# Causal cut of the diagonal tiles: a mask matmul on TensorE, or a select on GpSimd

## The chip, the cores and the metric

The kernel runs on one core of a Trainium2 chip. The metric is the device time in microseconds (us) of one execution; lower is better. The profile is one execution taken by the hardware profiler; its span runs from the first to the last instruction.

## What is computed

A token array of 2 batch rows x 1024 tokens x 128 features goes first through one attention layer of 16 heads of 8 features with its MLP (the opening of the kernel), and then through four decoder layers. Each of these has causal attention with 16 query heads and 4 key/value heads of 64 features and a mixture of 8 experts of which each token takes 2. Only the causal attention of the four layers is touched here:

```python
x = hidden_states
for l in range(L):                                   # L = 4, NH = 16, NKV = 4, HD = 64
    h = _rms(x, ln1_w[l])
    q, k, v = ...                                    # projections, rotary on q and k
    k = jnp.repeat(k, rep, axis=1); v = jnp.repeat(v, rep, axis=1)
    scores = jnp.einsum('bhqd,bhkd->bhqk', q, k) / jnp.sqrt(HD)
    scores = scores + causal_bias                    # 0 for k <= q, -1e9 for k > q
    attn = jax.nn.softmax(scores, axis=-1)
    out = jnp.einsum('bhqk,bhkd->bhqd', attn, v)
    x = jnp.clip(x + out.transpose(...).reshape(...) @ wo[l], -100, 100)
    x = jnp.clip(x + _moe(_rms(x, ln2_w[l]), ...), -100, 100)
```

## The kernel before

**Tiling.** A layer has `HEADS` = 8 passes: 4 key/value heads for each of 2 batch rows. A pass treats `GQ` = 4 query heads together. Its 1024 queries are 8 tiles of 128 (`t`), its keys 8 tiles of 128 (`kt`), and only `kt <= t` is computed: 36 steps a pass, of which 8 are diagonal (`kt == t`). Over 4 layers this is 1152 steps with 256 diagonal ones.

**A step.** `scores2` on TensorE writes the scores of 128 keys x (4 heads x 128 queries) into one of two PSUM banks `psS` with two matmuls (L1782, L1783); the row maximum is already among the operands. On a diagonal step a third matmul (L1785) adds the bf16 mask `maskk` through an identity, -1e9 where the key is later than the query. ScalarE takes the exponential (L1415) into `prob`, a ring of four SBUF buffers of 128x512 fp32. TensorE multiplies it by the values (`values`, L1799) into `psO`. GpSimd adds the tiles of a query tile up into `psum_k` for the denominator (L1217, shown as xw): one addition for each step with `kt > 0`. After the last step of a query tile TensorE spreads the sum with a matmul by ones (`denominator`, L1814), VectorE inverts it and scales (L2084, L2086), TensorE applies the output projection (`out_projection`, L1821) and VectorE adds the result (L2205). For `t == 0` the denominator reads `prob` directly.

**Beside it** runs work for the passes that follow: projections (L1725 to L1727), rotary sums on GpSimd (L1234), their low parts (L1243), and row maxima (L1754 with their own mask `maskq`, L1757, and the reductions L2110 on VectorE). These take the other four PSUM banks. After a layer's attention come the experts, which overlap its last pass.

**What sets the order.** Each engine runs its instructions in a fixed order. `network_order` describes every step as a stage with an engine, a cost in ns and the stages that it follows; `planned` walks through them as a list scheduler with 150 ns for a handover between engines and 110 ns for a turn of TensorE between 64-column work (kinds V and D) and the rest, and the program is written out in that order. So a changed cost or dependency moves the work of all engines. The opening is planned apart, and `opening_order` is not touched. In the tables of names, `S` is a step's scores on TensorE, its exponential on ScalarE and its addition on GpSimd; `V` the values, `D` the denominator, `O` the output projection, `M` the maxima.

**Waits.** `s_ex` counts exponentials, `s_su` GpSimd's additions, `s_pv` values, `s_qk` scores, `s_dn` denominators. An exponential waits for its scores and for the values and the addition of the step four before, which read the same buffer of `prob`.

## Time and profile before

| | us |
|---|---|
| median of 3 runs | 3364.86 |
| lowest and highest | 3364.70, 3366.26 |
| the profiled execution | 3365.88 |
| its span | 3364.0 |

The opening takes the first 640 us; the four layers follow. The profile is read from its share of busy time by engine, then by stretches within a layer, then by the chain of work that ended last, and last by the single instructions that the change removes or adds. A matmul's duration in the profile covers its way through the array, so that of matmuls that follow each other closely each one's own cost is the distance from one end to the next; the chain shows this distance.

### The profile page before, as it was taken

What the parts mean: (1) busy time and instruction counts of PE and PEld (TensorE: products, weight loads), DVE (VectorE), ACT (ScalarE), POOL (GpSimd) and SP (SyncE); (2) the same over time, 40 slices, a digit from 0 to 9 for tenths busy, and PEclk for the clock granted to TensorE, in tenths of its full rate; (3) what the DMA queues carried; (4) which work ended last, traced back from release to release, by engine and by line L of the source; (5) the groups of instructions that cost most, each with busy time, mean ns of one, the idle gap of its engine ahead of it and who ended that gap; (6) DMA issues with size and microseconds to landing.
All of it is one profiled execution on the core that took longest, in us unless ns stands there. A gap on an engine that the chain in (4) does not pass through costs nothing.

```text
span 3364.0 us, 51431 instructions
## 1 busy us (share of the span) xinstructions
PE 3165.4 (94%) x17792; PEld 2097.7 (62%) x17792; DVE 2568.0 (76%) x3764; ACT 1706.8 (51%) x3085; POOL 2009.9 (60%) x1573
## 2 busy tenths in 40 slices
PE   5999998799999999999999999999999999999998
PEld 3555554566666677666666776666667766666576
DVE  6778775777887777878876778778867888788667
ACT  4566667444435475444344755443446553443465
POOL 2101000378778665778776657787776577876765
PEclk8899999899999999999999999999999999999999
DMA  5433412333322155332231553232215532232153
GB/s 121 78 67 62 81 45 43 77 85 68 75 61 67 46 172 134 82 73 64 67 73 32 181 138 85 61 76 67 61 30 188 141 90 61 67 76 61 27 175 116
DMA packets 160401, 283.60 MB, mean 84 GB/s; under 512 B 32592, under 2 KB 64208, under 8 KB 159888
## 3 DMA queue, kind: packets, MB, share of 16 engines
q1 hardware_dynamic: 159632, 280.18, 33.4%
q8 instruction: 145, 2.38, 0.3%
q14 instruction: 112, 0.92, 0.1%
q10 hardware_dynamic: 512, 0.13, 0.0%
HBM read 88.47 MB, written 31.72 MB: 36 GB/s over the span
## 4 chain that ended last, share of the span: by engine, by line
PE 52%; DVE 6%; ACT 3%; issue 2%; POOL 1%; DMA 1%; SPq 0%; DVEq 0%; ACTq 0%
PE psA L1799 11%; PE psA L1782 7%; PE psA L1754 6%; PE psA L1783 5%; PE psA L1826 3%; PE psA L1827 3%; PE psA L1828 3%; PE psA L1814 3%; DVE rden L2084 2%; PE psA L1821 2%; DVE mxp L2110 2%; PE psA L1863 1%; PE psA L1757 1%; PE psA L1864 1%; PE psA L1865 1%
## 5 line engine op out<-in xcount | busy, mean ns | idle before, releaser
L1415 ACT ACTIVATE prob<-psA 128x512 f32<-128x512 f32 x1152 | 652.6, 595 | 1045.6 <-PE psA L1783 460.2
L1217 POOL TENSOR_TENSOR xw<-xw,prob 128x512 f32<-128x512 f32 x672 | 867.9, 1291 | 232.3 <-ACT prob L1415 158.5
L2110 DVE TENSOR_REDUCE mxp<-psA 128x1 f32<-128x512 f32 (+3 forms) x864 | 528.5, 663 | 57.1 <-PE psA L1754 35.2
L2084 DVE RECIPROCAL rden<-psA 128x256 f32<-128x256 f32 x256 | 448.8, 1753 | 131.9 <-PE psA L1814 125.5
L1782 PE MATMUL psA<-qs,ks 128*128 128x512 f32 x1152 | 524.8, 456 | 18.7 <-ACT prob L1415 17.4
L1754 PE MATMUL psA<-ks,qs 128*128 128x512 f32 (+3 forms) x1536 | 476.6, 387 | 11.8 <-DVE mxp L2110 5.7
L1251 POOL TENSOR_TENSOR hidl<-gate,hidh 128x512 fp32r<-128x512 f32 x256 | 331.2, 1302 | 211.4 <-ACT hidh L1470 209.6
L1783 PE MATMUL psA<-qs,ks 128*128 128x512 f32 x1152 | 454.6, 395 | 0.0
L1217 POOL TENSOR_TENSOR xw<-prob 128x512 f32<-128x512 f32 x224 | 287.7, 1284 | 274.0 <-issue 129.8
L2032 DVE TENSOR_REDUCE mxp<-psA 128x1 f32<-128x1024 f32 x256 | 304.7, 1220 | 83.7 <-PE psA L1590 82.7
L1334 ACT ACTIVATE pr<-psA 128x512 f32<-128x512 f32 x512 | 274.3, 602 | 140.1 <-PE psA L1609 122.9
L1754 PEld LDWEIGHTS psA<-ks,qs 128*128 128x128 f32 x1536 | 270.7, 193 | 84.8 <-issue 31.8
L1782 PEld LDWEIGHTS psA<-qs,ks 128*128 128x128 f32 x1152 | 221.1, 192 | 140.0 <-issue 67.4
L1799 PE MATMUL psA<-prob,vv 128*64 128x256 f32 x2304 | 292.2, 387 | 6.5 <-DVE inner L2205 3.7
L1799 PE MATMUL psA<-prob,outer 128*64 128x256 f32 x2304 | 293.6, 386 | 5.0 <-DVE inner L2205 5.0
L2110 DVE TENSOR_REDUCE mxq<-psA 128x1 f32<-128x384 f32 (+3 forms) x352 | 209.7, 637 | 105.0 <-PE psA L1757 103.0
L1234 POOL TENSOR_TENSOR rab<-rab,rbp 128x512 f32<-128x512 f32 x192 | 247.4, 1303 | 36.5 <-DMA rbp<-rab 36.5
L2236 DVE TENSOR_TENSOR gate<-psA,spread 128x512 f32<-128x512 f32 x256 | 175.9, 687 | 101.5 <-ACT psA L1464 100.4
L1163 POOL TENSOR_TENSOR feat<-feat,smr 128x1024 f32<-128x1024 f32 x16 | 30.6, 1915 | 360.3 <-DVE smr L2015 360.3
L1783 PEld LDWEIGHTS psA<-qs,ks 128*128 128x128 f32 x1152 | 219.0, 190 | 21.3
L1826 PE MATMUL psA<-xh,eh 128*128 128x512 f32 x512 | 211.4, 413 | 17.9 <-DVE gate L2236 10.4
L1799 PEld LDWEIGHTS psA<-prob,vv 128*64 128x64 f32 x2304 | 155.1, 137 | 104.1 <-issue 25.6
(222 smaller groups left out, 5839.0 us busy)
## 6 DMA issues: line engine op xcount, KB each, us to landing
qs<-normed SPq DMA_DIRECT2D x256, 256.0 KB, 4.1
rbp<-rab SPq DMA_DIRECT2D x256, 192.0 KB, 3.5
spread<-routing_weights SPq DMA_DIRECT2D x128, 256.0 KB, 3.6
qs<-qs SPq DMA_DIRECT2D x64, 256.0 KB, 3.2
expert_weight_halves<-eh SPq DMA_DIRECT2D x32, 384.0 KB, 2.5
expert_weight_halves<-el SPq DMA_DIRECT2D x32, 384.0 KB, 3.6
eh<-expert_weight_halves SPq DMA_DIRECT2D x32, 384.0 KB, 3.2
el<-expert_weight_halves SPq DMA_DIRECT2D x32, 384.0 KB, 3.9
```

The source lines that it names most:

```text
L1217: g.tensor_tensor(psum_k[:, t % 2, :], before, prob[:, i % 4, :], ALU.add).then_inc(s_su, 1 if kt > 1 else 2 + (t == 1))
L1251: g.tensor_tensor(hidl[:, n % 3, :], gate[:, n % GATES, :], hidh[:, n % 3, :], ALU.subtract).then_inc(s_hl, 1)
L1334: act(pr1[:, j % 2, h, :], psS1[:, n % 3, :], ACT.Exp).then_inc(s_ex1, 1)
L1415: act(prob[:, k % 4, :], psS[:, k % 2, :], ACT.Exp, scale=float(HD) ** -0.5).then_inc(s_ex, 1)
L1754: ins = mm(bank[:, i, :], qs1[b][:, c, h + i, t % TPC * P:(t % TPC + 1) * P], ks[b][:, 0, k0:k1], start=(i == 0), stop=not diagonal)
L1782: mm(psS[:, i % 2, :], ks[b][:, 0, tile], qs1[b][:, c, :, qs], start=True, stop=False)
L1783: ins = mm(psS[:, i % 2, :], ks[b][:, 1, tile], qs2[b][:, c, :, qs], start=False, stop=(kt < t))
L1799: ins = mm(psO[t % 2][q * HD:(q + 1) * HD, 0:256], vv[b][:, kt, g * HD:(g + 1) * HD], prob[:, i % 4, q * 256:(q + 1) * 256], start=(kt == ...
L1826: mm(dst, eh[held(w)][:, w0:w0 + P], xh[:, cs], start=True, stop=False)
L2032: vec.tensor_reduce(mxp1[:, p % 2, c, h * 4 + t:h * 4 + t + 1], pair("M", p, c, t, h), AX.X, ALU.max).then_inc(s_mx1, 1)
L2084: vec.reciprocal(rden[:, :], psO[t % 2][:, 256:512]).then_inc(s_rd, 1)
L2110: vec.tensor_reduce(dst, bank, AX.X, ALU.max).then_inc(s_mr, 1)
```

## The change

The diagonal step loses its mask matmul (and `maskk` its setup). After the exponential GpSimd sets the entries of later keys to zero in place, with an `affine_select` over the 128 x (4 x 128) tile: a new stage `Sd` for each of the 256 diagonal steps, with a cost of 900 in the plan. The values of a diagonal step, its addition, and the denominator of `t == 0` now wait for this select through a new semaphore `s_sd2`. The row maximum (`maskq`) stays as it is.

```diff
-        stage("tensor", ("S", l, n, t, kt), 440 + 100 * (kt == t), ("land", ("J", l, n, t // TPC)) if kt == 0 else None,
+        stage("tensor", ("S", l, n, t, kt), 440, ("land", ("J", l, n, t // TPC)) if kt == 0 else None,
               back("scalar", "S", 2), *first)
         stage("scalar", ("S", l, n, t, kt), 600, ("tensor", ("S", l, n, t, kt)), back("tensor", "V", 4), back("gpsimd", "S", 4))
-        stage("gpsimd", ("S", l, n, t, kt), 1390 * (kt > 0), ("scalar", ("S", l, n, t, kt)),
-              tile("tensor", "D", 2) if kt == 1 else None)
+        if kt == t:
+            stage("gpsimd", ("Sd", l, n, t), 900, ("scalar", ("S", l, n, t, t)))
+        whole = ("gpsimd", ("Sd", l, n, t)) if kt == t else ("scalar", ("S", l, n, t, kt))
+        stage("gpsimd", ("S", l, n, t, kt), 1390 * (kt > 0), whole, tile("tensor", "D", 2) if kt == 1 else None)
         if t == 0:
-            stage("tensor", ("D", l, n, t), 500, ("scalar", ("S", l, n, 0, 0)), tile("vector", "O", 2), *early)
-        stage("tensor", ("V", l, n, t, kt), 460, ("scalar", ("S", l, n, t, kt)),
+            stage("tensor", ("D", l, n, t), 500, whole, tile("vector", "O", 2), *early)
+        stage("tensor", ("V", l, n, t, kt), 460, whole,
...
+                elif what == "Sd":
+                    l, n, t = i
+                    it, k = l * HEADS + n, TRI[t] + t
+                    g_.wait_ge(s_ex, it * TRI[TPB] + k + 5)
+                    cut = prob[:, k % 4, :].rearrange("p (h n) -> p h n", h=GQ)
+                    g.affine_select(out=cut, in_=cut, compare_op=ALU.is_ge, fill=0.0, base=0,
+                                    pattern=[[0, GQ], [1, P]], channel_multiplier=-1).then_inc(s_sd2, 1)
...
+                    if kt == t:
+                        g_.wait_ge(s_sd2, it * TPB + t + 1)
...
-                ins = mm(psS[:, i % 2, :], ks[b][:, 1, tile], qs2[b][:, c, :, qs], start=False, stop=(kt < t))
-                if kt == t:
-                    ins = mm(psS[:, i % 2, :], identb[:, :], maskk[:, :].unsqueeze(1).broadcast_to([P, GQ, P]), start=False, stop=True)
-                ins.then_inc(s_qk, 1)
+                mm(psS[:, i % 2, :], ks[b][:, 1, tile], qs2[b][:, c, :, qs], start=False, stop=True).then_inc(s_qk, 1)
...
                 t_.wait_ge(s_ex, it * TRI[TPB] + i + 5)
+                if kt == t:
+                    t_.wait_ge(s_sd2, it * TPB + t + 1)
...
-                    t_.wait_ge(s_ex, it * TRI[TPB] + 5)
+                    t_.wait_ge(s_sd2, it * TPB + 1)
```

The plan comes out in another order. GpSimd in the second layer, pass 5, before: query tiles 4 and 5 (L1217 additions, L1234 rotary sums, L1243 low parts).

```order
L1217 TENSOR_TENSOR xw<-prob 128x512
L1217 TENSOR_TENSOR xw<-xw,prob 128x512 x3
L1234 TENSOR_TENSOR rab<-rab,rbp 128x512 x2
L1217 TENSOR_TENSOR xw<-prob 128x512
L1217 TENSOR_TENSOR xw<-xw,prob 128x512 x4
L1243 TENSOR_TENSOR qs_0<-rab,normed 128x512 x2
```

The same place after the change. L1208 is the select; the additions are now L1225, the rotary sums L1242, the low parts L1251.

```order
L1225 TENSOR_TENSOR xw<-prob 128x512
L1225 TENSOR_TENSOR xw<-xw,prob 128x512 x2
L1208 AFFINE_SELECT prob<-prob 128x512
L1225 TENSOR_TENSOR xw<-xw,prob 128x512
L1242 TENSOR_TENSOR rab<-rab,rbp 128x512
L1225 TENSOR_TENSOR xw<-prob 128x512
L1225 TENSOR_TENSOR xw<-xw,prob 128x512
L1242 TENSOR_TENSOR rab<-rab,rbp 128x512
L1225 TENSOR_TENSOR xw<-xw,prob 128x512 x2
L1208 AFFINE_SELECT prob<-prob 128x512
L1225 TENSOR_TENSOR xw<-xw,prob 128x512
L1251 TENSOR_TENSOR qs_0<-rab,normed 128x512
```

Each query tile's last addition has a select right ahead of it, and rotary sums that stood in pairs are spread between additions.

TensorE at the diagonal step of query tile 4 in the same pass, before: from the scores of key tile 4 to the values (L1799) that read them.

```order
L1782 MATMUL psA<-qs_1,ks 128x512
L1783 MATMUL psA<-qs_1,ks 128x512
L1785 MATMUL psA<-maskk,identb 128x512
L1782 MATMUL psA<-qs_1,ks 128x512
L1783 MATMUL psA<-qs_1,ks 128x512
L1821 MATMUL psA<-wos,att 128x128 x2
L1754 MATMUL psA<-ks,qs_0 128x384
L1757 MATMUL psA<-maskq,identb 128x128
L1799 MATMUL psA<-prob,vv 64x256 x12
L1782 MATMUL psA<-qs_1,ks 128x512
```

The end of the same piece after the change (scores are L1790 and L1791, maxima L1762 and L1765, values L1806, denominator L1821 there). The diagonal scores stand 22 rows above the values, with the output projection, three further steps of scores and seven pieces of maxima between them.

```order
L1762 MATMUL psA<-ks,qs_0 128x384
L1765 MATMUL psA<-maskq,identb 128x128
L1762 MATMUL psA<-ks,qs_0 128x512
L1765 MATMUL psA<-maskq,identb 128x128
L1762 MATMUL psA<-ks,qs_0 128x512
L1765 MATMUL psA<-maskq,identb 128x128
L1762 MATMUL psA<-ks,qs_0 128x512
L1765 MATMUL psA<-maskq,identb 128x128
L1762 MATMUL psA<-ks,qs_0 128x512
L1765 MATMUL psA<-maskq,identb 128x128
L1806 MATMUL psA<-prob,vv 64x256 x12
L1821 MATMUL psA<-xw,ones 64x256 x2
```

The values of the diagonal step moved back behind other work, and the denominator joined them in one run of 64-column matmuls.

## Rows read from the trace of the kernel before

**Rows 1.** The page: busy time by engine, then shares in 40 slices.

```profile
PE 3165.4 (94%) x17792; PEld 2097.7 (62%) x17792; DVE 2568.0 (76%) x3764; ACT 1706.8 (51%) x3085; POOL 2009.9 (60%) x1573
...
PE   5999998799999999999999999999999999999998
...
PEclk8899999899999999999999999999999999999999
```

**Rows 2.** Busy time in two stretches of attention: start:end, length, PE, PEld, DVE, ACT, POOL.

```profile
1340.00:1840.00 500.00, 484.10 (x2982) 316.95 (x2981) 388.84 (x596) 215.20 (x394) 374.23 (x294) 1.00 0.27 63
```

```profile
2000.00:2480.00 480.00, 464.60 (x2823) 308.07 (x2821) 384.70 (x588) 207.94 (x377) 356.77 (x280) 1.00 0.28 65
```

**Rows 3.** The chain that ended last within 1340 to 1840 us, shares by line.

```profile
by line: PE psA L1799 24.7%; PE psA L1782 14.8%; PE psA L1783 11.6%; PE psA L1754 11.5%; PE psA L1814 5.5%; DVE rden L2084 3.8%; PE psA L1821 3.8%; DVE mxp L2110 3.4%; PE psA L1757 2.5%; PE psA L1785 2.5%; issue 2.3%; PE psA L1725 1.8%; PE 
```

**Rows 4.** The mask matmul L1785 within 1340 to 1840 us: PE busy and count.

```profile
1340.00:1840.00 500.00, 24.27 (x62) 5.99 (x62) 1.00 0.27 63
```

**Rows 5.** The chain within 1400 to 1440 us in time: start, own cost in us, what.

```profile
1407.30 0.28 PE psA L1782
1407.58 0.24 PE psA L1783
1407.82 0.23 PE psA L1785
...
1427.81 1.88 PE psA L1799 x16
1429.69 0.43 PE psA L1814 x4
1430.12 0.43 PE psA L1782
1430.55 0.24 PE psA L1783
1430.79 0.23 PE psA L1782
```

**Rows 6.** GpSimd by line and form: count, busy us, mean ns, idle before.

```profile
L1217 POOL TENSOR_TENSOR xw<-xw,prob 128x512 f32<-128x512 f32 x672 | 867.9, 1291 | 232.3 <-ACT prob L1415 158.5 <-POOL xw L1217 1.3
...
L1190 POOL COPY outer<-vtok 128x256 f32<-128x256 f32 x8 | 3.2, 398 | 30.3 <-PE psA L1620 21.8 <-ACT vtok L1301 8.4
...
L1179 POOL MEMSET order<- 128x1 f32 x8 | 0.3, 99 | 0.0
...
L1149 POOL TENSOR_SCALAR_AFFINE_SELECT ident<-ident 128x128 f32<-128x128 f32 x1 | 0.3, 292 | 0.2 <-POOL ident L1147 0.2
...
L1185 POOL TENSOR_SCALAR_AFFINE_SELECT maskk<-maskk 128x128 bf16<-128x128 bf16 x1 | 0.3, 292 | 0.0
```

**Rows 7.** In order of time: start us, us, engine, line, idle before and its releaser.

```profile
863.83 1.08 ACT L1415 ACTIVATE prob<-psA 128x512 f32<-128x512 f32 x2 [4.86 <-PE psA L1799]
864.51 1.29 POOL L1217 TENSOR_TENSOR xw<-xw,prob 128x512 f32<-128x512 f32 x1 [4.11 <-ACT prob L1415]
...
870.61 0.39 PE L1785 MATMUL psA<-maskk,identb 128*128 128x512 bf16 x1
...
871.04 0.60 ACT L1415 ACTIVATE prob<-psA 128x512 f32<-128x512 f32 x1 [0.87 <-PE psA L1785]
```

**Rows 8.** Who waited for whom over the whole span: us, times, longest.

```profile
ACT prob L1415 <- PE psA L1799: 323.1, 139, 5.1
...
PEld psA L1821 <- DVE att L2086: 45.0, 55, 1.6
...
ACT prob L1415 <- POOL xw L1217: 28.9, 39, 2.6
...
PEld psA L1799 <- ACT prob L1415: 28.9, 72, 1.4
```

More of the change, by code:

```diff
@@ L641, in network_order @@
              "Ew", "Eh", "El", "Es", "Er", "Hf", "Hw", "Hh", "Hl", "Si", "Y", "Ug", "Uu", "Aw", "Wa", "Wb",
-             "W", "K", "H", "R", "Q", "J", "A", "X", "L", "D", "O", "V", "S", "P", "M", "Zk", "Za", "Zb", "Zs", "Zv", "Zd", "Zi", "Zr", "Zo"]
+             "W", "K", "H", "R", "Q", "J", "A", "X", "L", "D", "O", "V", "Sd", "S", "P", "M", "Zk", "Za", "Zb", "Zs", "Zv", "Zd", "Zi", "Zr", "Zo"]
     return planned(plan, kinds, 150, 150, "VD", 110, {"vector": 120})
@@ L690, in program @@
         maskq = sb("maskq", [P, P], BF16)
-        maskk = sb("maskk", [P, P], BF16)
         ones64 = sb("ones64", [P, HD])
@@ L841, in program @@
         s_rw = [sem(f"max2_in_stack_{c}") for c in range(NCH)]
+        s_sd2 = sem("diagonal_cut")
         s_qk, s_ex, s_su, s_pv = sem("scores2"), sem("exp2"), sem("probabilities_summed"), sem("pv2")
@@ L861, in program @@
         PV_FREE = 2 * TPB + 2
-        N_CS2 = 4 + E + 3
+        N_CS2 = 3 + E + 2
         ROWS_DONE = scaled(4, 3) + 1
@@ L1174, in opening @@
                         g.memset(maskq[:, :], 0.0).then_inc(s_cs2, 1)
-                        g.memset(maskk[:, :], 0.0).then_inc(s_cs2, 1)
                         g.memset(ones64[:, :], 1.0).then_inc(s_cs2, 1)
@@ L1179, in opening @@
                             g.memset(order[:, e:e + 1], float(E - e)).then_inc(s_cs2, 1)
-                        g_.wait_ge(s_cs2, 4 + E)
+                        g_.wait_ge(s_cs2, 3 + E)
                         g.affine_select(out=identb[:, :], in_=identb[:, :], compare_op=ALU.not_equal, fill=1.0, base=0,
@@ L1184, in opening @@
                                         pattern=[[-1, P]], channel_multiplier=1).then_inc(s_cs2, 1)
-                        g.affine_select(out=maskk[:, :], in_=maskk[:, :], compare_op=ALU.is_ge, fill=NEG, base=0,
-                                        pattern=[[1, P]], channel_multiplier=-1).then_inc(s_cs2, 1)
                     if p > 1:
```

## The prediction

> **What bounds the kernel now.** I read the page first, for the share of each engine. TensorE is busy 94% of the span and at full granted clock in nearly all slices after the opening; no other engine is above 76% [rows 1]. An average can hide a stage with another limit, so the next view is the busy time by stretches inside the attention of two layers. In 1340 to 1840 us TensorE works 484.1 of 500 us (97%), VectorE 388.8 (78%), GpSimd 374.2 (75%), ScalarE 215.2 (43%) [rows 2]; in 2000 to 2480 us the shares are 97, 80, 74 and 43%. So here TensorE has 3% of idle time and GpSimd 25%. Busy matmuls may still be waiting ones, so the third view is the chain that ended last in this stretch: mostly matmuls, with VectorE's reciprocal at 3.8% and its maxima at 3.4%, GpSimd nowhere among the first lines, and the mask matmul L1785 itself at 2.5% [rows 3]. This is the picture of an engine that is the bound by its own issue: time taken from it comes off the end, unless something else steps in at once.
>
> **The matmuls removed.** There are 256 of them (4 layers x 8 passes x 8 diagonal steps). Their duration in the windows is 24.27 us for 62 [rows 4], 0.39 us each, but that is the way through the array; in the chain each costs 0.23 us, as the score matmuls beside it do [rows 5]. 256 x 0.232 = 59.4 us of TensorE's time (0.232 is the middle distance between the ends of L1783 and L1785 over the 256 pairs, [rows 5] rounds it). How much of that is on the path: L1785 has 2.5% of 500 us in the chain [rows 3], 12.5 us, where its 62 instances [rows 4] cost 62 x 0.232 = 14.4 us. So 87% is on the path: 59.4 x 0.87 = 51.6 us. The rest ran in the shadow of a chain through VectorE. I take 51.6, and 59.4 as the upper bound.
>
> What another rule would make of this term: the Trainium skill, "TensorE: Matmul & The Clock Gate", section "Back-to-back issue gap", gives about 131 ns for each 512-column matmul in a sustained stream of weight loads and matmuls, against about 216 ns for an isolated one. By 131 ns the term would be 256 x 0.131 = 34 us, by 216 ns 55 us. The chain says 0.23 us [rows 5], so the trace stands against the lower figure, and near the higher one.
>
> **Fewer turns.** TensorE pays for going between 64-column work (values and denominators) and 128-column work. In the chain, 16 matmuls L1799 cost 1.88 us and the 4 of L1814 behind them 0.43; at the latter's pace of 0.1075 the 16 are worth 1.72, so entering costs 0.16. The first L1782 after them costs 0.43 where the next ones cost 0.24, so leaving costs 0.19 [rows 5]. That is 0.175 us a turn. Counting through the planned orders, the four layers have 722 turns before and 658 after, because denominators join the values (as in the second pair of pieces of the order above). 64 x 0.175 = 11.2 us less. This falls on the bound engine too; I take it whole. Its bounds are 0, if the gathered work then waits for its inputs, and 11.2.
>
> **What GpSimd gets.** 256 selects of 128x512 fp32. The trace has selects of 128x128 only, 292 ns each in fp32 and in bf16 alike [rows 6]. Four times that is 1.17 us and is the upper bound by proportion, if all of it were per element; an addition with two inputs of the full size takes 1.29 [rows 6] and is the far end. From below, a one-input copy of 128x256 takes 398 ns [rows 6]: twice that is 0.80. With the fixed part counted once the select lies between: from 292 at 128 elements and the copy's fixed part (about 0.1 us, as the memset of one column [rows 6] shows) comes (292 - 100) x 4 + 100 = 0.87 us. I take 0.87, range 0.6 to 1.29. GpSimd then has 256 x 0.87 = 223 us more, 2010 + 223 = 2233 us. In the first stretch [rows 2] that is 62 x 0.87 = 54 us more: 428 of some 485 us, 88%. It is the second busiest engine, still with slack. With 1.29 it would be 454 of 485, 94%: there it is nearly a bound.
>
> **The wait added.** The path from diagonal scores to their values gets longer by the select. An exponential takes 0.60 us; one starts 0.04 after its scores (870.61 + 0.39 against 871.04), and an addition 0.08 after its exponential (863.83 + 0.60 against 864.51) [rows 7]. So scores to values was about 0.64 plus a handover of 0.1 to 0.3; with the select 0.64 + 0.08 + 0.87 + 0.2 = 1.8 us, and 3.1 if GpSimd is just inside an addition. The plan has room for this: laying the costs of [rows 5] along TensorE's order, the work between diagonal scores and their values is 4.9 us on average before and 6.0 after. Before, 61 of 256 diagonals have less than 2.5 us; after, 8 have less than 3 (the last pass of each layer, two each, 1.4 and 2 us). So TensorE should wait at a handful of places, 4 x 0.4 plus the odd addition in front: 2 us. Behind such a waiting L1799 stands everything that TensorE does, which is why the count matters.
>
> Two more places get later. A buffer of `prob` is freed only by the values, and the exponential four steps on waits for that: ScalarE already waits 323 us for L1799 and 29 us for GpSimd's additions [rows 8]. It is 43% busy, and its scores lie two deep in PSUM, so a delay of about 1 us in one step out of four or five reaches TensorE only where it has no maxima or projections to do, in the last pass of a layer. And the last addition of a query tile comes 0.87 us later, then the denominator, the reciprocal and L1821, where TensorE waits 45 us now [rows 8]. The plan moved these too. I add 3 us for both, with 0 and 60 as bounds (60: a quarter of a select for each diagonal). On SyncE nothing is added; GpSimd's rotary sums (whose stores go by SyncE) are moved behind a select or an addition here and there, a delay of about 1 us in work planned a whole pass ahead. The setup loses a memset and a select of GpSimd in the opening, under other work: nothing.
>
> **The sum.** Against the profiled execution's span: 3364.0 - 51.6 - 11.2 + 2 + 3 = 3306.2 us. The median of the runs is 0.9 above the span, which gives 3307 us, 1.7% faster. All terms good: 3364.9 - 59.4 - 11.2 = 3294. Half of the gain eaten: 3335.
>
> **The rivals.**
> (a) *The gain is half eaten by dependencies* (20%). TensorE's 97% leaves VectorE at 80% and GpSimd at 88%, in fixed orders made from rough costs: the plan counts 1.39 us for an addition that takes 1.29 and 0.90 for a select that I take at 0.87. With 60 us of slack taken from TensorE, misfits that were hidden show up: 30 us, 3335. For it speaks the 13% of L1785 outside the chain; against it, that real GpSimd work is cheaper than planned.
> (b) *GpSimd becomes the bound* (7%): slower than before. If the select costs as much as an addition (1.29), GpSimd stands at 94% and each diagonal's select is queued behind additions; the values wait, and with them the ring of four `prob` buffers, the exponentials and the next scores. The break-even is (51.6 + 11.2)/256 = 0.245 us of TensorE wait for each diagonal. At 0.5 us each the time is 3364.9 - 62.8 + 128 = 3430. For it: ScalarE's 323 us of waits on L1799; against: the 292 ns for 128 columns and the room of over 3 us at 248 of 256 places.
> (c) *The matmul was hidden anyway* (6%): the chain only seems to run through it, and VectorE's maxima and reciprocals with GpSimd's sums set the pace at the place where the layers hand over. Then 3360 to 3370. Against it speaks the 2.5% on the line itself [rows 3].
> (d) *The low price of a 512-column matmul* (2%): if one removed gives back less than its distance, say 0.13 us, since the weight load of the neighbour then comes to light, the term is 33 x 0.87 = 29 us and the time 3330.
>
> **Chances.** Forecast 65%, around 3307 (3294 to 3320 alone). With (a), (d) and the gap between them the time is under 3345 in 87%. A measurement of this kernel can tell 0.2% (6.7 us) from no change: faster 87%, same 6%, slower 7%. The range takes in the full gain with some luck in the new order (3288) and reaches through (a) to 3345; what is left out is mostly (b) and (c).
>
> **What would show it.** Right: no L1785; in stretches of a layer's attention TensorE still at 96 to 97% busy and each layer's attention 14 to 16 us shorter; the select's row with 256 at about 0.87 us; GpSimd at 2230 us (67% of the span); few and short waits of L1806 (the values) for the select, under 10 us in all; turns down, so that the chain's mean for 64-column runs falls. Wrong: TensorE at 93% or less in these stretches and the waits list led on TensorE by the select (b), or by VectorE's lines with GpSimd's additions behind them (a); a select of 1.2 us or more; waits of ScalarE on the values well above 323 us with scores behind them.

## The result, and the profile after

| | before | after |
|---|---|---|
| median of the runs, us | 3364.78 | 3397.14 |
| lowest and highest | 3363.17, 3366.26 | 3393.60, 3403.18 |
| ratio, 95% interval | | 1.0098 [1.0081, 1.0116] |
| span of the profiled execution | 3364.0 | 3391.9 |

The change makes the kernel 32 us (1.0%) slower. The forecast was 3307 us. Of all runs below one, of `plan_440_neither`, fell into a slower state of the chip (3842 us at a granted clock of 0.74), and its time is left out of that kernel's median.

The page of the kernel after, busy time by engine and the granted clock in 40 slices, answers to [rows 1]. The clock is as before. TensorE has 256 matmuls less and is 44 us less busy, but its share fell from 94 to 92%. GpSimd has 64%, nowhere near a bound.

```profile
PE 3121.4 (92%) x17536; PEld 2088.5 (62%) x17536; DVE 2584.7 (76%) x3764; ACT 1709.1 (50%) x3085; POOL 2156.0 (64%) x1827
...
PEclk8899999899999999999999999999999999999999
```

Busy time in the two stretches of [rows 2] (start:end, length, PE, PEld, DVE, ACT, POOL): TensorE has 469.5 of 500 us and 453.4 of 480, 94% where it had 97%, and does less in the same time.

```profile
1340.00:1840.00 500.00, 469.48 (x2888) 313.78 (x2887) 395.21 (x606) 215.74 (x392) 403.49 (x351) 1.00 0.27 64
2000.00:2480.00 480.00, 453.36 (x2743) 308.14 (x2743) 382.58 (x583) 210.91 (x382) 387.59 (x335) 1.00 0.29 68
```

The select in the view of its line: 256 of them at 0.64 us. Of those that waited for it, only additions are named, 3.2 us in all. No values (L1806) waited for it.

```profile
L1208 POOL TENSOR_SCALAR_AFFINE_SELECT prob<-prob x256: 624/634/1093, 638.4 to 3228.5; 128x512 f32<-128x512 f32 x128
...
  POOL xw L1225: 3.2, 11
```

The waits (engine and line, what it waited for: us in total, times, longest) show where TensorE stands now. First the kernel after, then the lines of before that answer and that [rows 8] has not:

```profile
ACT prob L1423 <- PE psA L1806: 476.0, 190, 5.4
...
PEld psA L1790 <- ACT prob L1423: 97.2, 145, 2.3
...
PEld psA L1828 <- DVE att L2093: 66.5, 71, 1.6
...
PE psA L1790 <- ACT prob L1423: 45.4, 78, 2.1
...
PE psA L1828 <- DVE att L2093: 43.0, 65, 1.1
...
PEld psA L1806 <- ACT prob L1423: 30.8, 79, 1.3
```

```profile
PEld psA L1782 <- ACT prob L1415: 51.0, 92, 1.7
...
PE psA L1821 <- DVE att L2086: 31.5, 36, 1.2
...
PE psA L1782 <- ACT prob L1415: 17.4, 42, 1.5
```

Scores (L1790) wait for an exponential: they need one of two PSUM banks, and the exponential of two steps before must have read it. Those waits went from 51.0 and 17.4 us (weight load and matmul) to 97.2 and 45.4. The output projection (L1828, before L1821) waits for the divided values `att`: from 45.0 and 31.5 to 66.5 and 43.0. No select stands in either wait, and no output projection was edited.

The chain that ended last in 1340 to 1840 us, by line, answers to [rows 3]: the reciprocal L2091 has 5.9% where it had 3.8%.

```profile
by line: PE psA L1806 23.6%; PE psA L1790 13.4%; PE psA L1762 10.9%; PE psA L1791 10.3%; DVE rden L2091 5.9%; PE psA L1821 4.6%; PE psA L1828 3.9%; DVE mxp L2117 2.7%; issue 2.4%; DMA qs<-mrow 2.2%; PE psA L1765 2.2%; PE psA L1733 1.9%; PE 
```

In order of time (start, own cost, what) this chain repeats with each pass, 63.9 us apart. Its pieces off TensorE in one pass are one exponential, two key copies of ScalarE, the low part of the keys on VectorE (L2219, 1.5 us), two reciprocals, and maxima around the second of them. Without the maxima:

```profile
1522.04 0.61 ACT prob L1423
...
1526.06 0.62 ACT ks L1448
...
1526.70 0.63 ACT ks L1449
...
1527.36 1.50 DVE ks L2219
...
1545.88 1.77 DVE rden L2091
...
1550.09 1.68 DVE rden L2091
...
1585.91 0.60 ACT prob L1423
```

Before, a pass took 63.3 us. The same view has one key copy in full, one exponential and one reciprocal in it, with maxima on both sides of the reciprocal, and not the low part of the keys:

```profile
1518.87 0.63 ACT ks L1441
...
1519.52 0.61 ACT prob L1415
...
1541.77 1.68 DVE rden L2084
...
1582.16 0.63 ACT ks L1441
```

The new reciprocal closely, in the chain from 1540 to 1556 us: the denominator (L1821), its reciprocal, the division, the output projection, each right behind the other. This path takes 2.3 us. The one reciprocal of before (1541.77) has maxima and values behind it in the chain, no output projection.

```profile
1545.41 0.46 PE psA L1821 x4
1545.86 0.02 issue
1545.88 1.77 DVE rden L2091
1547.65 0.02 issue
1547.68 0.43 DVE att L2093
1548.11 0.04 issue
1548.15 0.71 PE psA L1828 x4
```

TensorE does not stand still for all of it. In the view of all instructions of this stretch it works on maxima and scores from 1545.77 to 1547.49, and waits 0.66 us for the division:

```profile
1545.77 0.96 PE L1762 MATMUL psA<-ks,qs 128*128 128x512 f32 x3
...
1547.26 0.23 PE L1765 MATMUL psA<-maskq,identb 128*128 128x128 bf16 x1
...
1548.15 0.71 PE L1828 MATMUL psA<-wos,att 128*128 128x128 f32 x4 [0.66 <-DVE att L2093]
```

So the order has put 1.6 us of work between denominator and output projection, where the path asks for 2.3.

**A measure for all runs.** For each matmul I took the distance from the end of the one before it to its own end. What exceeds the lower quartile of all runs for the same pair of shapes I call *stall*, the rest *issue*. Over the whole span, in us (a sum over the matmul records, good to some 3 us; the two records of a 64-column matmul count as one; some 240 us of stall at other matmuls, in the opening and the experts above all, are in it in each kernel):

| kernel | stall | issue | stall at scores | output proj. | maxima | values |
|---|---|---|---|---|---|---|
| before | 379 | 2952 | 37 | 42 | 26 | 16 |
| after | 473 | 2886 | 94 | 60 | 42 | 12 |

TensorE did get its 66 us back (2952 to 2886; the prediction had 59.4 + 11.2 = 70.6). It then stands still for 94 us more.

Where in a layer: in the second layer, of 679.6 us before and 685.9 after, the four steady passes give +0.6 each, the one behind them +1.2, and the last, which has little work beside it, +3.1 (55.7 to 58.8 us between its first and last scores). The prediction wanted each layer 14 to 16 us shorter.

### The profile page after: what moved, and what is told of

Read it like the earlier page. It is cut to its first block, busy times and chain, and to the rows that moved or that the text cites. A ratio compares the mean times of both kernels' runs of the same rounds, so it can differ in the third digit from the quotient of the medians.

```text
span 3391.9 us, 51433 instructions
## 1 busy us (share of the span) xinstructions
PE 3121.4 (92%) x17536; PEld 2088.5 (62%) x17536; DVE 2584.7 (76%) x3764; ACT 1709.1 (50%) x3085; POOL 2156.0 (64%) x1827
## 4 chain that ended last, share of the span: by engine, by line
PE 74%; DVE 12%; ACT 5%; DMA 3%; issue 3%; POOL 1%; SPq 1%; ACTq 0%; DVEq 0%; POOLq 0%
PE psA L1806 15%; PE psA L1790 8%; PE psA L1762 7%; PE psA L1791 6%; PE psA L1598 4%; PE psA L1617 4%; DVE rden L2091 4%; PE psA L1628 4%; PE psA L1833 3%; PE psA L1821 3%; PE psA L1834 3%; PE psA L1835 3%; PE psA L1828 2%; DVE mxp L2117 2%; DMA qs<-mrow 2%
## 5 line engine op out<-in xcount | busy, mean ns | idle before, releaser
L1225 POOL TENSOR_TENSOR xw<-xw,prob 128x512 f32<-128x512 f32 x672 | 869.8, 1294 | 124.4 <-ACT prob L1423 49.3
L2091 DVE RECIPROCAL rden<-psA 128x256 f32<-128x256 f32 x256 | 449.2, 1755 | 179.5 <-PE psA L1821 170.2
L1790 PE MATMUL psA<-qs,ks 128*128 128x512 f32 x1152 | 520.3, 452 | 60.5 <-ACT prob L1423 45.4
L1762 PE MATMUL psA<-ks,qs 128*128 128x512 f32 (+3 forms) x1536 | 459.2, 380 | 24.2 <-DVE ks L2219 10.5
L1791 PE MATMUL psA<-qs,ks 128*128 128x512 f32 x1152 | 454.3, 394 | 0.0
L1225 POOL TENSOR_TENSOR xw<-prob 128x512 f32<-128x512 f32 x224 | 286.5, 1279 | 171.0 <-issue 138.2
L1762 PEld LDWEIGHTS psA<-ks,qs 128*128 128x128 f32 x1536 | 273.2, 193 | 119.9 <-DVE mxp L2117 39.1
L1790 PEld LDWEIGHTS psA<-qs,ks 128*128 128x128 f32 x1152 | 220.5, 191 | 199.1 <-ACT prob L1423 97.2
L1806 PE MATMUL psA<-prob,vv 128*64 128x256 f32 x2304 | 291.1, 387 | 5.0 <-ACT prob L1423 2.5
L1806 PE MATMUL psA<-prob,outer 128*64 128x256 f32 x2304 | 291.3, 386 | 2.7 <-DVE inner L2212 2.7
L1242 POOL TENSOR_TENSOR rab<-rab,rbp 128x512 f32<-128x512 f32 x192 | 245.3, 1281 | 34.9 <-DMA rbp<-rab 34.9
L1791 PEld LDWEIGHTS psA<-qs,ks 128*128 128x128 f32 x1152 | 219.4, 190 | 18.4
L1208 POOL TENSOR_SCALAR_AFFINE_SELECT prob<-prob 128x512 f32<-128x512 f32 x256 | 162.6, 639 | 94.7 <-ACT prob L1423 94.7
```

The costliest lines, as they stand in the source:

```text
L1225: g.tensor_tensor(psum_k[:, t % 2, :], before, prob[:, i % 4, :], ALU.add).then_inc(s_su, 1 if kt > 1 else 2 + (t == 1))
L1762: ins = mm(bank[:, i, :], qs1[b][:, c, h + i, t % TPC * P:(t % TPC + 1) * P], ks[b][:, 0, k0:k1], start=(i == 0), stop=not diagonal)
L1790: mm(psS[:, i % 2, :], ks[b][:, 0, tile], qs1[b][:, c, :, qs], start=True, stop=False)
L1791: mm(psS[:, i % 2, :], ks[b][:, 1, tile], qs2[b][:, c, :, qs], start=False, stop=True).then_inc(s_qk, 1)
L1806: ins = mm(psO[t % 2][q * HD:(q + 1) * HD, 0:256], vv[b][:, kt, g * HD:(g + 1) * HD], prob[:, i % 4, q * 256:(q + 1) * 256], start=(kt == ...
L2091: vec.reciprocal(rden[:, :], psO[t % 2][:, 256:512]).then_inc(s_rd, 1)
```

## The experiments

The time behind "against" is the median of before in runs made beside those of the kernel; where none is named it is that of the kernel above. A verdict rests on the ratio with its 95% interval.

### Order and work apart

The diff changes the work (mask matmul out, select in) and, through the plan, the order of all engines. These four kernels separate the two. In the old order the select stands on GpSimd right ahead of the addition of its own step; in the new order without a select its place is dropped. "Neither" has no mask matmul and no select, so the causal cut inside the diagonal tiles is left out.

`old_order`: the plan's stages as before, selects put in by hand.

```diff
+NETWORK["gpsimd"] = [x for item in NETWORK["gpsimd"]
+                     for x in ([("Sd", *item[1:4])] if item[0] == "S" and item[3] == item[4] else []) + [item]]
```

> The change, but every engine in the order of the kernel before; GpSimd's select stands right ahead of the diagonal step's addition. Theory 1 (the new plan's order is what costs: TensorE's stalls grow because values and scores were regrouped): the gain of the mask matmuls shows, less the waits at the 61 diagonal places with under 2.5 us of cover, some 0.5 us each: 3364.8 - 52 + 30 = 3343, faster than before. Theory 2 (the select's latency costs, through the wait of the values and the ring of four prob buffers, in any order): not faster, 3390 or more, since this order makes no room for the select.

3472.5 us against 3364.2, 1.0311 [1.0294, 1.0327].

`new_order_mask`: the kernel before, mask matmul and all, with the plan's stages of after; `Sd` is dropped from the finished order.

```diff
+NETWORK["gpsimd"] = [item for item in NETWORK["gpsimd"] if item[0] != "Sd"]
```

> The kernel before with its mask matmul and without any select, in the order of the changed kernel. Theory 1 (order): as slow as the changed kernel or slower, about 3397 plus up to 52 for the matmuls put back: 3400 to 3450. Theory 2 (select): the order alone costs nothing and saves 11 us of turns: 3350 to 3370.

3408.95 us, 1.0125 [1.0105, 1.0144].

`old_order_neither` and `new_order_neither`: the mask matmul out of before and out of the kernel above.

```diff
...
-                if kt == t:
-                    ins = mm(psS[:, i % 2, :], identb[:, :], maskk[:, :].unsqueeze(1).broadcast_to([P, GQ, P]), start=False, stop=True)
...
```

> The order of before, with neither the mask matmul nor a select: the causal cut inside the diagonal tiles is left out, so the output is not the reference's. Both theories: the bare value of the mask matmuls in this order, 3364.8 - 52 = 3313. If it stays near 3365, the matmuls were hidden in this order and the first term of the prediction falls.

3338.9 us, 0.9922 [0.9902, 0.9942].

> The order of the changed kernel with neither mask matmul nor select (the causal cut inside the diagonal tiles is left out). Theory 1 (order): stays near the changed kernel, 3380 to 3397. Theory 2 (select): 3302, the forecast without any wait.

3385.8 us, 1.0059 [1.0043, 1.0076].

Together with the two kernels of the case, and the third order found below (recosted), in us:

| order | mask | neither | select | mask matmuls are worth | select costs |
|---|---|---|---|---|---|
| before's | 3364 | 3339 | 3472 | 25 | 133 |
| after's | 3409 | 3386 | 3397 | 23 | 11 |
| recosted | 3334 | 3291 | 3322 | 42 | 31 |

**The new order alone costs 45 us** (3364 to 3409), with not one instruction of a step added or removed. Removing the mask matmuls then brings 23 and the select takes 11: 45 - 23 + 11 = 33, the measured 32. The change of the work, in an order that gives the select room, is a gain of 12 us (3409 to 3397); without that room it is a loss of 108. Each ratio is known to about 6 us to either side and a difference of two to 8 or 9, so these 11 and 12 us are told from nothing, but their size is rough. The 45, 108 and 133 are far outside.

The stalls say the same. Taking the matmuls out took their whole 59 us from the issue and gave 33 and 28 of them back as stalls. The new order saved 7 us of turns and added 55 of stalls, 41 of them at the scores.

| kernel | stall | issue | stall at scores | output proj. | maxima | values |
|---|---|---|---|---|---|---|
| old_order_neither | 412 | 2893 | 56 | 50 | 25 | 21 |
| old_order | 538 | 2893 | 86 | 23 | 38 | 122 |
| new_order_mask | 434 | 2945 | 78 | 52 | 30 | 10 |
| new_order_neither | 462 | 2886 | 91 | 60 | 34 | 11 |

Why the select needs room, from the waits of old_order: the values wait for the select directly, 68 times, and this is most of the 122 us.

```profile
PE psA L1806 <- POOL prob L1208: 84.8, 68, 3.4
```

And the waits of new_order_mask, which has the work of before and the order of after. At the scores its lines are those of after (97.2 and 45.4), not those of before (51.0 and 17.4); at the output projection they lie between (after 66.5 and 43.0, before 45.0 and 31.5):

```profile
PEld psA L1785 <- ACT prob L1418: 95.7, 141, 2.3
...
PEld psA L1824 <- DVE att L2089: 57.2, 68, 1.6
...
PE psA L1785 <- ACT prob L1418: 44.0, 73, 2.1
...
PE psA L1824 <- DVE att L2089: 35.9, 60, 1.1
```

### Which edit of the plan makes the bad order

`plan_440_neither`: of the two edits only the cost of the diagonal scores, 540 to 440, and no stage `Sd`; no mask and no select, to stand beside 3339 and 3386.

```diff
-        stage("tensor", ("S", l, n, t, kt), 440 + 100 * (kt == t), ...
+        stage("tensor", ("S", l, n, t, kt), 440 + 0 * (kt == t), ...
...
```

> Neither mask nor select (the causal cut inside the diagonal tiles is left out), in the order that the plan gives when only the diagonal scores are costed 440 instead of 540 and no select stands in it. To be set against the same work in the order of before (3339) and in that of the change (3386). If the cost edit is what turned the order bad: near 3386. If it is the select's stage with its 900 and its handovers: 3330 to 3345.

3313.1 us against 3364.6, 0.985 [0.9832, 0.9868]. That order is better than before's by 26 us, so the edit of the cost alone does not make the order bad. With that cost, adding the stage `Sd` and what hangs on it turns 3313 into 3386, 73 us. The stage with the old cost of 540 was not run.

`select_640`: the select at its measured price.

```diff
-            stage("gpsimd", ("Sd", l, n, t), 900, ("scalar", ("S", l, n, t, t)))
+            stage("gpsimd", ("Sd", l, n, t), 640, ("scalar", ("S", l, n, t, t)))
```

> The changed kernel with the select costed 640 in the plan, as the trace has it, instead of 900. Theory 'the wrong cost spoils the order': the order gets back to that of before, 3340 to 3370. Theory 'the order is a lottery in which a single true cost among rough ones decides nothing': between 3370 and 3420, not clearly better than 3397.

3395.7 us, 1.0087 [1.0072, 1.0102]. A wrong price of the select, taken by itself, isn't it either.

`recosted_after`: the costs of scores, select and addition set nearer to the traces (the select still above its 0.64 us), and three of the plan's settings changed: handover, turn and slack of VectorE.

```diff
-        stage("tensor", ("S", l, n, t, kt), 440, ...
+        stage("tensor", ("S", l, n, t, kt), 480, ...
...
-            stage("gpsimd", ("Sd", l, n, t), 900, ...
+            stage("gpsimd", ("Sd", l, n, t), 750, ...
...
-        stage("gpsimd", ("S", l, n, t, kt), 1390 * (kt > 0), ...
+        stage("gpsimd", ("S", l, n, t, kt), 1340 * (kt > 0), ...
...
-    return planned(plan, kinds, 150, 150, "VD", 110, {"vector": 120})
+    return planned(plan, kinds, 120, 150, "VD", 150, {"vector": 60})
```

> The changed kernel's work with a plan whose costs are nearer to the trace: scores 480, select 750, additions 1340, a turn of TensorE 150 (its own 175 in the chain), handover 120, slack of VectorE 60. Theory 'the change is good and its order bad': TensorE's stalls return to 2 to 3 us a pass and the time goes below the kernel before, 3250 to 3330. Theory 'the select itself costs': not below 3364.

3322.3 us, 0.987 [0.9855, 0.9884].

`recosted_before`: the same costs and settings with the mask, whose diagonal scores are 480 + 230.

> The kernel before (mask matmul, no select) with the same new costs and settings of the plan, its diagonal scores at 480 + 230 as the chain shows them. It tells what of recosted_after's gain is the plan's and what the change's. Theory 'the change is worth its 25 us less the select's 11 in a good order': recosted_before is 10 to 50 us slower than recosted_after. Theory 'the change is worth nothing': the two are the same within 7 us.

3367.8 us, 1.0008 [0.9999, 1.0018]. The same recosting took 75 us from after and nothing from before (its 3 us more can't be told from none). Which of the six changed numbers does it was not tried. So with the change the plan can be 45 us better than without it (3322 against 3368), or 32 worse (3397 against 3365).

### Which dependencies carry the loss

`before_short_divide` and `after_short_divide`: VectorE copies the denominators (0.4 us) instead of taking their reciprocal (1.76); so the division is left out, and VectorE has some 300 us less work too. This shortens the path of the chain piece above in both kernels.

```diff
-                vec.reciprocal(rden[:, :], psO[t % 2][:, 256:512]).then_inc(s_rd, 1)
+                vec.tensor_copy(rden[:, :], psO[t % 2][:, 256:512]).then_inc(s_rd, 1)
```

> The kernel before with the same short copy in place of the reciprocal (output not the reference's). Theory 'reciprocal': gains 10 to 25 us (10.6 us short in its order, and a lighter VectorE), 3340 to 3355, level with after_short_divide. Theory 'exponentials and ring': the same gain, but after_short_divide stays 25 to 35 us above it.

3313.7 us against 3367.5, 0.9838 [0.9824, 0.9853].

> The changed kernel with VectorE's reciprocal (L2091, 1.75 us) replaced by a copy of the same tile (about 0.4 us), so the division is wrong and the output not the reference's. Laying the costs of the chain along TensorE's order, the work between a denominator and its output projection is under the 2.6 us that the reciprocal's path takes at 25 places of the order before (10.6 us short in all) and at 90 of the new one (46.5 us short). Theory 'the new order starves TensorE behind the reciprocal': this kernel gains 45 to 60 us, to about 3345, and is no slower than before_short_divide. Theory 'TensorE starves behind the exponentials and the ring of prob buffers': it gains 10 to 25 us and stays 25 to 35 us above before_short_divide.

3335.3 us, 0.9905 [0.9887, 0.9922]. Before gained 54 us and after 62. The gap between them shrinks from 32 to 22: the path over the reciprocals is a third of the loss at most. The stalls at the scores stay (40 and 107 us).

`after_five_buffers`, `old_order_five_buffers`: five buffers of `prob`, order unchanged.

```diff
-        prob, wst, wvst = over("prob", [P, 4, 512], F32, ...
+        prob, wst, wvst = over("prob", [P, 5, 512], F32, ...
...
-                    act(prob[:, k % 4, :], psS[:, k % 2, :], ACT.Exp, ...
+                    act(prob[:, n_ex % 5, :], psS[:, k % 2, :], ACT.Exp, ...
```

> The changed kernel in its own order with five prob buffers instead of four: an exponential waits for the values and the addition of five steps before. Theory 'ring': most of the growth of TensorE's waits for exponentials (L1790: 68 us before, 143 after) goes, 3397 to about 3330-3350. Theory 'order behind the reciprocal': 3385 to 3397.

3375.6 us, 1.002 [1.0011, 1.003].

> The select in the order of the kernel before (3472 with four buffers, 3339 without a select), now with five prob buffers. If the select's cost of 133 us in that order runs through the ring (late values hold a buffer, the exponentials wait): most of it goes, 3360 to 3400. If it is TensorE waiting at the values for GpSimd's queue (the trace shows L1806 waiting for the select): 3455 to 3472.

3443.7 us, 1.023 [1.0209, 1.0252]. A fifth buffer is worth 21 and 29 us: the exponentials' wait for a free buffer costs time in both orders. Before was not run with five buffers, so it isn't shown that the ring is part of the difference between before and after; and most of the waits of scores for exponentials are left (88.8 us of weight loads where after has 97.2).

`recosted_five`: five buffers, known to the plan as well, with the costs of recosted_after.

> The changed kernel, the costs of recosted_after, and five prob buffers, planned as five. Five buffers gave 21 us in the changed kernel's own order and 29 in the old one. If that adds to the recosted order: 3295 to 3305. If the recosted order has no waits left at the ring: 3318 to 3326.

3319.6 us against 3366.1, 0.986 [0.9845, 0.9874]: 3 us less than recosted_after, which can't be told from none. The fifth buffer finds nothing left to gain there; since the plan knew of it, this is another order too, and the ring alone was not isolated.

### Which engine's order

`rotary_together`: the rotary sums of GpSimd, which the new plan spreads between additions, gathered three in a row again. My theory then was that the key copies of ScalarE wait for the last of these sums (50.3 us in after, 14.0 before) and hold the exponentials behind them.

```diff
+placed = []
+for item in NETWORK["gpsimd"]:
+    if item[0] == "A" and item[4] > 0:
+        continue
+    placed += [(*item[:4], w) for w in range(3)] if item[0] == "A" else [item]
+NETWORK["gpsimd"] = placed
```

> The changed kernel with one thing moved: GpSimd does the three rotary sums of a half pass (L1242) one behind the other where the first stands, since all three wait for the same DMA, instead of spreading them between additions and selects. Theory 'GpSimd's place for the last sum': ScalarE's copies of the keys no longer stand in front of an exponential waiting for it (50 us of waits, 14 before), TensorE's waits at scores behind them (28 us) fall under 10, and the time falls by 15 to 30 us, to 3367 to 3382. Rival 'the additions and selects that now come up to 2.6 us later cost as much': 3390 or more.

3412.8 us against 3366.1, 1.0137 [1.012, 1.0154]: 16 us worse than after. The theory fell, and the trace says at which step. The edit did what it was meant to, as the key copies no longer wait for the sums:

```profile
ACT ks L1454 <- POOL rab L1248: 1.0, 2, 0.6
```

But the stalls at scores whose exponential stands right behind a key copy are 28 us, as in after (29). It is not the wait for GpSimd that makes these copies stand in the way.

`new_order_old_gpsimd`: the work of before; TensorE, ScalarE and VectorE in the new order, GpSimd and SyncE in the old one.

```diff
+EARLIER = order_before()
+for engine in ("gpsimd", "sync", "land"):
+    NETWORK[engine] = EARLIER[engine]
```

> Mask matmul, no select; TensorE, ScalarE and VectorE in the changed kernel's order, GpSimd and SyncE in that of the kernel before. Beside new_order_mask (3409) only GpSimd's and SyncE's order differs, beside the kernel before (3365) that of the three others. Theory 'GpSimd's order is the cause': 3365 to 3380. Theory 'the cause is in the order of scores, values, denominators and outputs on TensorE with ScalarE and VectorE': 3400 to 3415.

3418.3 us against 3366.25, 1.0151 [1.0136, 1.0167]. With GpSimd's old order the three other engines are no better than with its new one (3409), and TensorE's waits at the scores stay at 89.9 and 43.7 us. So the new order of TensorE, ScalarE and VectorE is enough for the loss. The reverse, GpSimd's new order beside the old one of the others, was not run.

### The third order, and the best kernel

`recosted_order_mask` and `recosted_order_neither`: the order of recosted_after held fixed, with the mask matmul and without, as above.

> The mask matmul and no select, in the order of recosted_after (3322). By the two orders measured so far mask matmuls are worth 25 us (3364 to 3339; 3409 to 3386). Theory 'their value is 25 in any order': recosted_order_neither + 25. Theory 'in an order with few other waits they are worth nearer to their 59': + 40 to 59, about 3350 to 3370.

3333.6 us against 3366.1, 0.9901 [0.9886, 0.9916].

> Neither mask nor select in the order of recosted_after (the causal cut inside the diagonal tiles is left out). What the select costs where the order makes room for it: theory 'cover decides' (12 diagonals with under 2.9 us of cover, against 73 in the order of before, where it cost 133): 3307 to 3317, 5 to 15 us below recosted_after. Rival 'it costs by GpSimd's load, 163 us more in any order': 30 us or more below.

3291.2 us, 0.9776 [0.9761, 0.9791]. These are the third row of the table. Here the mask matmuls are worth 42 us: of the 59 us that left the issue only some 20 came back as stalls (367 to 387). The select costs 31, far more than the 5 to 15 expected from the room at the values, and no values wait for it here. With it the exponentials wait longer for the values (367 to 471 us) and the scores longer for the exponentials (weight load and matmul: 32.9 and 16.2 us to 48.9 and 30.3). So room between diagonal scores and values is needed, but it does not set the price of the select alone. The change of the work is worth 11 again. And before's own work runs 31 us faster in an order that was drawn for the select than in its own: the old order was no optimum.

Part of that is turns of TensorE. Recosting prices a turn at 150 instead of 110, and the turns in the traces fall from 722 to 522 (506 in recosted_before). TensorE's issue falls with them, from 2952 us to 2927 in recosted_order_mask and 2925 in recosted_before. The two differ in the stall, 367 and 407 us where before has 379, and so in time: 3334 and 3368 us.

`recosted2_after`: the costs of recosted_after, other settings, chosen among plans by how far cover falls short where a matmul depends on another engine: output projections less than 2.6 us behind their denominator (before at 25 places, 10.6 us in all; after 90, 46.5; recosted_after 52, 27; here 44, 23), scores too close behind those of two steps before, and values too close behind a diagonal's scores. The edit is shown against recosted_after.

```diff
-    return planned(plan, kinds, 120, 150, "VD", 150, {"vector": 60})
+    return planned(plan, kinds, 210, 200, "VD", 150, {"vector": 180})
```

> The changed kernel with the costs of recosted_after and other settings of the plan (handover 210 and 200 more from TensorE, slack of VectorE 180 instead of 120, 150 and 60). Theory 'the costs of scores, additions and turns carry the gain': 3315 to 3330, as recosted_after. Theory 'each order is a draw of its own': anywhere from 3310 to 3390.

3299.6 us against 3366.3, 0.9795 [0.9779, 0.9812]: the best kernel that computes the reference, 65 us below before and 98 below after. Its page and stretch, with the work of after: TensorE is back at 97% (483 of 500), and a steady pass takes 60.3 us where it took 63.9. It lies below both ranges expected (3315 to 3330 if the costs carry the gain, 3310 to 3390 if each order is a draw), and one kernel picked this way does not show that the count of short places picks good orders: recosted_after has 27 us of it where before has 10.6, and is 42 us faster.

```profile
span 3299.8 us, 51433 instructions
...
PE 3091.7 (94%) x17536; PEld 2094.8 (63%) x17536; DVE 2587.5 (78%) x3764; ACT 1711.8 (52%) x3085; POOL 2164.3 (66%) x1827
```

```profile
1340.00:1840.00 500.00, 483.25 (x2981) 329.49 (x2982) 401.94 (x608) 231.19 (x422) 423.62 (x365) 0.99 0.30 72
```

Its waits: scores behind exponentials a third of after's 97.2 and 45.4 us.

```profile
PEld psA L1828 <- DVE att L2093: 49.7, 74, 1.4
...
PEld psA L1790 <- ACT prob L1423: 31.2, 48, 1.9
...
PE psA L1828 <- DVE att L2093: 23.0, 52, 1.2
...
PE psA L1790 <- ACT prob L1423: 16.2, 22, 1.8
```

## Why the prediction was wrong

**The bound was read half.** TensorE at 97% of a stretch [rows 2] does not say that time taken from it comes off the end. A busy matmul in this profile can be a waiting one, as the prediction itself said; by the distances a steady pass of before has 3.1 us of stall in its 63.3 (after 5.8 in 63.9). That is 5% in which TensorE already stood waiting, and at such a place time taken from it comes back as a wait. Taking only the mask matmuls out shows it: 33 and 28 of 59 us came back.

**The matmuls removed** (51.6 forecast). Their own cost was right: 59.2 us left the issue of TensorE (2952 to 2893). What came off the end was 25, 23 and 42 us in three orders. The share of a line in the chain [rows 3] says that the chain goes through it. It doesn't say how much shorter the next chain is, and half of the gain came back as stalls elsewhere. This term was 28 us too good in the order that was measured (51.6 against 23). This is rival (a) in kind, and half is what it gave; it had 20%.

**Fewer turns** (11.2 forecast). 7 us in the issue (2952 to 2945 in new_order_mask). The gathering that saved them sits in an order that costs 55 us in stalls: the bound of 0 that the prediction gave for this was far too kind.

**"The plan moved these too. I add 3 us for both"** is the step that failed. The new order entered the sum with its turns, -11.2 us, and with a share of these 3 us (bounds 0 and 60) for two places that get later: the ring of `prob`, and the denominator with its reciprocal. The order as such had no term. Measured alone, with the work of before, it costs 45 us where the sum had -11.2, and its stalls grow at scores, output projections and maxima. The miss adds up: 56 us for the order, 28 for the mask matmuls, 6 for the select (11 against 2 + 3), together the 90 between 3307 and 3397. I had laid the cover along the new order for one pair only, the diagonal's scores and their values, where it is better than before. The same count for denominator and output projection, made after the result, gives 25 short places before and 90 after. That number needs only the planned order and the durations in the trace of before, and here it points the right way. It is only a third of the loss, as the kernels with the short divide show.

**The select.** 0.64 us, not 0.87, inside the range of 0.6 to 1.29; GpSimd 2156 us, not 2233. The wait of the values for it is nil in the new order, as forecast (2 us). But its real price is not that wait: 11 us in this order, 31 in the recosted one, 133 where it has no room.

**The signs.** TensorE fell to 94%, between the 96 and the 93 named. What came true of the signs of being wrong is the last: ScalarE's waits for the values went from 323 to 476 us, with scores behind them. The waits on TensorE are led by the exponentials, a sign that was named neither for (a) nor for (b).

**The rivals.** (b), GpSimd as the bound: false, 64% busy and a cheap select. Its mechanism, values that wait for the select and hold all of TensorE, is real and was seen in old_order; the new plan had removed it. (c) and (d) would end at no change or a gain. None of the rivals was "the order as such is worse", and that was the case. Slower had 7%, all of it for (b). A redraw of the whole program, whose quality the prediction had checked at one pair of stages, should have had more.

**What stays open.** Why just this order of TensorE, ScalarE and VectorE makes scores wait. The trace offers a reading: of 94 us at the scores 46 stand where the exponential that must free their bank was held by other ScalarE work (28.5 us behind the key copies L1449, 14 behind a table load of 1.28 us), against 18 in before (7 and 11). A further 23 us, 2 in before, stand where the exponential ran right behind another one. No experiment moved the key copies of ScalarE alone, so this is argued and not shown; what `rotary_together` shows is that without their wait for GpSimd the stalls behind them stay. Nor is it shown that true costs make a better plan: recosting helped after by 75 us and before by none, and the order that it drew for before is 34 us worse than the one drawn for the select (3368 against 3334, same work). The part of luck in such a draw is as large as the effect sought, or larger.

## What to carry to other kernels

Where a planner writes the order, measure a change of the work in a fixed order too, with the new order and the old work as the control: here the change was worth -12 us and its new order +45. After such a change redraw the plan (costs, handover, slack) before judging it; and before running it, lay the durations along the new order for every pair in which the bound engine depends on another, not only for the pair that the change adds; such a count can warn, but it did not rank the orders here. A line's share in the critical chain was more than what its removal gave (25, 23 and 42 of 52 us), in all three orders.

## What was not expected of the hardware

A select of 128x512 fp32 in place takes GpSimd 0.64 us (624 to 1093 ns), half of an addition of that shape (1.29) and far below four times the 292 ns of the 128x128 ones [rows 6]: about 116 ns for each 128 columns more. The spacing of the removed matmuls in the score stream was confirmed by taking them out: 59.2 us for 256, 0.23 us each. The lower figure of 131 ns in the Trainium skill, "TensorE: Matmul & The Clock Gate", section "Back-to-back issue gap", is not what this stream shows; what came off the end per matmul (0.10, 0.09 and 0.17 us in the orders of before, after and recosted_after) is its 0.23 us less what came back as stalls.
